# One list of pieces for a decoder layer's attention, with the work before and after it put between

## The reference, cut to what matters

```python
qkv = tgt @ qkv_w.T + qkv_b                      # tgt = layernorm(x), per entry 512 x 128
q, k, v = split(qkv, 3)
scores = (q k^T) * sqrt(128); all but the diagonal = -inf; attn = softmax(scores)
x1 = ln(tgt + (attn @ v) @ sa_out_w.T + sa_out_b) * ln1_g + ln1_b
# cross attention, 8 heads of 16, over 154 context rows per entry
ca = softmax(heads(x1 @ wq.T + bq) heads(mem @ wk.T + bk)^T / 4) heads(mem @ wv.T + bv)
x2 = ln(x1 + ca @ mha_out_w.T + mha_out_b) * ln2_g + ln2_b
x3 = ln(x2 + relu(x2 @ lin1_w.T + lin1_b) @ lin2_w.T + lin2_b) * ln3_g + ln3_b
x = x + tanh(g_xattn[3]) * x3
```

## Time and profile before

| what | value |
|---|---|
| median of 3 runs | 1736.38 us (1730.84 to 1736.41) |
| the profiled execution | 1737.62 us, its span 1735.8 us |
| PE busy over the span | 1430.0 us (82%) |
| DVE busy | 1154.2 us (66%) |
| GpSimd busy | 816.3 us (47%) |
| ACT busy | 767.0 us (44%) |
| granted PE clock, mean | 0.907 |

### The profile page before, as it was taken

One profiled execution on the slowest core, in us unless ns is written; L12 is line 12 of the kernel. 1 busy time (PEld: TensorE's weight loads), 2 busy tenths in 40 slices (PEclk: granted clock), 3 DMA queues, 4 the chain that ended last, 5 costly groups with the idle time before them and its releaser, 6 DMA issues.

```text
span 1735.8 us, 36462 instructions
## 1 busy us (share of the span) xinstructions
PE 1430.0 (82%) x13597; PEld 973.2 (56%) x13597; DVE 1154.2 (66%) x3020; ACT 767.0 (44%) x1520; POOL 816.3 (47%) x1236
## 2 busy tenths in 40 slices
PE   3999999999999986766798599869984885669997
PEld 2777777777777674644665255524443333425545
DVE  4888688877877764554856667554556565787754
ACT  3777677767766653411233355443212542201111
POOL 4789889978766872561336632000001301143330
PEclk9999999999999997965899899989986887879898
DMA  7332321211211202320000000000000000000000
GB/s 268 88 95 87 91 87 48 59 42 46 53 49 42 61 22 77 111 97 0 1 1 1 12 5 2 1 1 1 1 1 0 1 1 1 1 1 1 7 7 13
DMA packets 35477, 64.27 MB, mean 37 GB/s; under 512 B 7536, under 2 KB 25043, under 8 KB 34148
## 3 DMA queue, kind: packets, MB, share of 16 engines
q1 hardware_dynamic: 33831, 59.82, 11.6%
q0 software_dynamic: 1472, 2.12, 0.4%
HBM read 30.64 MB, written 12.66 MB: 25 GB/s over the span
## 4 chain that ended last, share of the span: by engine, by line
PE 62%; DVE 20%; ACT 6%; POOL 5%; issue 5%; DMA 2%; SPq 0%; ACTq 0%; DVEq 0%; POOLq 0%
PE banks L505 17%; PE banks L745 6%; PE banks L773 5%; PE banks L734 5%; PE banks L2145 4%; DVE xn L451 2%; PE banks L2131 2%; PE banks L480 2%; ACT work L932 2%; PE banks L2838 2%; PE banks L2098 1%; DVE norm_room L415 1%; PE banks L2781 1%; DMA work<-work 1%; POOL work L1040 1%
## 5 line engine op out<-in xcount | busy, mean ns | idle before, releaser
L1040 POOL TENSOR_TENSOR work<-work 128x512 bf16<-128x512 f32 (+1 forms) x512 | 359.6, 726 | 74.1 <-ACT work L932 73.3
L817 DVE TENSOR_REDUCE work<-banks 128x1 f32<-128x666 f32 x256 | 216.3, 845 | 67.6 <-PE banks L734 65.9
L445 POOL TENSOR_TENSOR norm_room<-norm_room,minus_half 128x4 f32<-128x4 f32 x48 | 50.2, 1046 | 408.3 <-DVE norm_room L420 392.9
L939 ACT ACTIVATE work<-banks,work 128x666 f32<-128x666 f32 x256 | 208.3, 814 | 36.5 <-DVE work L817 28.5
L932 ACT ACTIVATE work<-banks 128x512 f32<-128x512 f32 x256 | 152.9, 597 | 142.0 <-PE banks L745 141.7
L734 PE MATMUL banks<-work 128*128 128x512 bf16 (+1 forms) x1024 | 187.2, 305 | 6.8 <-DMA work<-work 6.4
L745 PE MATMUL banks<-const,work 128*128 128x128 f32 x1024 | 158.7, 278 | 14.7 <-ACT work L932 11.6
L505 PE MATMUL banks<-work,weights_b 128*128 128x512 bf16 (+1 forms) x840 | 159.6, 349 | 11.7 <-DVE work L2473 4.6
L734 PEld LDWEIGHTS banks<-work 128*128 128x128 bf16 x1024 | 95.6, 98 | 85.4 <-DMA work<-work 7.6
L773 PE MATMUL banks<-work 128*128 128x65 bf16 (+1 forms) x3840 | 136.5, 192 | 3.4 <-POOL work L1040 1.8
L480 PE MATMUL banks<-const,xn 128*128 128x128 f32 x176 | 39.4, 365 | 117.4 <-DVE xn L451 79.0
(11 more groups left out here) (441 smaller groups left out, 3231.7 us busy)
## 6 DMA issues: line engine op xcount, KB each, us to landing
work<-work SPq DMA_DIRECT2D x128, 166.5 KB, 2.9
sorted<-in_pads SPq DMA_DIRECT2D x10, 838.5 KB
weights_b<-in_weights SPq DMA_DIRECT2D x1, 4120.0 KB, 23.7
work<-scratch SPq DMA_DIRECT2D x64, 64.0 KB, 2.0
weights_b<-in_weights SPq DMA_DIRECT2D x1, 2824.0 KB, 9.4
weights_a<-in_weights SPq DMA_DIRECT2D x1, 2056.0 KB, 8.4
weights_a<-in_weights SPq DMA_DIRECT2D x1, 2050.0 KB, 10.1
work<-work SPq DMA_DIRECT2D x32, 64.0 KB, 1.9
```

Of the source, the lines that this page charges most:

```text
L817: ve.tensor_reduce(self.neg_max[i % 4], self.slot[i % 2][:, 0:KEYS0], AX_X, ALU.max, negate=True).then_inc(self.mark("max"))
L939: ac.activation(self.probs[i % 3], self.slot[i % 2][:, 0:KEYS0], ACT.Exp, bias=self.neg_max[i % 4]).then_inc(self.mark("exp"))
L1040: po.tensor_tensor(parts[:, :, :, 0], exact, parts[:, :, :, 1], ALU.subtract).then_inc(self.mark(event, i - 3))
```

## The change

Stage 6 becomes one list. `decoder_items` gives positions to all pieces of the layer: entry 0's first part at -4 to -2.9; for entries 1 to 3 the same pieces (`ahead`) from 2b - 2.0 on, 0.085 apart, so within the attention of the entry before; and for each unit, behind its output product at u + 2.56, the second norm, the feed-forward, the third norm and the sum into x (`measure2` to `close`), so within the attention of the next units. The router of entry 0 stands at 5.1 to 8.0. GpSimd walks the same list now.

In the pieces themselves: the bias of q and k comes into PSUM by a small bf16 matmul (`lead`, `in_bias6`) and ACT copies q and k out; the values are projected as columns, so that they need no transposes; the softmax's share goes into one scalar_tensor_tensor per tile with the residual; the gain and bias of the first two norms go into ACT's copy of the transposes (per-partition scale and shift), and for the rows themselves to GpSimd (`gain1`, `gain2`, `residual`, `x_base`), with the later biases added in the same pass; the third norm's gain, bias and gate are folded into two scalar_tensor_tensor per tile (`close`). All this works on halves of entries behind the attention. In stage 6 scores use two banks (0 and 1) in place of three; bank 2 serves the side work. `parts7` and its neighbours become one buffer per entry, of which stage 7 clears three on GpSimd at its start. In stage 4 the order of the pieces is what it was.

```diff
@@ context_memory
+        a.score_banks = 3 if heads == 16 else 2
@@ context_items
-        out, n = [], 2 * a.steps
+        out, n = [(-3.0, "key", 0, 0, 0), (-3.0, "key", 1, 0, 0), (-2.9, "query", 0, 0, 0), (-1.0, "out_bias", 7, 0, 0)], 2 * a.steps
+        for g in range(GROUPS):
+            out += [(-2.0 + 0.2 * g, "key_spread", g, 0, 0), (-1.9 + 0.2 * g, "rows", 0, g, 3 + g)]
+        if a.stage == 6:
+            out = self.decoder_items()
...
@@ context_pe, in the loop over the items (context_ac and context_ve likewise)
+            elif s == 6:
+                self.decoder_item_pe(pe, what, u, c)
...
@@ after context_ve
+    def key_bank(self, a, g, n):
+        return (2 * g + n + 5) % 8 if a.stage == 4 else 3 + (2 * g + n) % 4
@@ decoder
+    def decoder_items(self):
+        def ahead(b, at, step):
+            pieces = (("project", 0, 0), ("project", 1, 1), ("values6", 0, 2), ("dots", 0, 3), ("exp6", 0, 3.5), ("delta", 0, 4.5),
+                      ("attend", 0, 5), ("first", 0, 6), ("scale1", 0, 9), ("turn1", 0, 11))
+            return [(at + step * n, what, b, c, 0) for what, c, n in pieces]
+        out = [(-4.0, "start", 0, 0, 0)] + ahead(0, -4.0, 0.1)
+        out += [(-3.66, "key", 0, 0, 0), (-3.64, "key", 1, 0, 0), (-3.52, "out_bias", 6, 0, 0)]
+        out += [(-3.38 + 0.02 * g, "key_spread", g, 0, 0) for g in range(GROUPS)] + [(-3.3, "heads", 0, 0, 0)]
+        out += [(-2.8, "query", 0, 0, 0), (-1.0, "prepare", 0, 0, 0)] + [(-2.6 + 0.1 * g, "rows", 0, g, 3 + g) for g in range(GROUPS)]
+        for b in range(BATCH):
+            out += [(2 * b + 0.3 if b == 0 else 2 * b - 1.0, "gain1", b, 0, 0), (2 * b + 1.5, "x_base", b, 0, 0)]
+            if b:
+                out += [(2 * b - 2.1, "residual", b, 0, 0), (2 * b - 1.4, "heads", b, 0, 0)] + ahead(b, 2 * b - 2.0, 0.085)
+        for at, what in ((1.3, "measure"), (1.6, "scale"), (1.8, "turn")):
+            out.append((at, what, 5, BATCH - 1, 0))
+        for u in range(2 * BATCH):
+            for what, c, at in (("measure2", 0, 0.03), ("scale2", 0, 0.2), ("turn2", 0, 0.28), ("gain2", 0, 0.34), ("up", 0, 0.38), ("up", 1, 0.43),
+                                ("up", 2, 0.48), ("up", 3, 0.53), ("down", 0, 0.74), ("measure3", 0, 0.93), ("close", 0, 1.12)):
+                out.append((u + 2.56 + at, what, u, c, 0))
+            if u % 2 and u < 2 * BATCH - 1:
+                out += [(u + 2.56 + at, what, 6, u // 2, 0) for what, at in (("measure", 1.2), ("scale", 1.4), ("turn", 1.52))]
+        out += [(5.1, "squares", 0, 0, 0), (5.2, "logits", 0, 0, 0)] + [(5.4 + 0.2 * n, "router", 0, n, 0) for n in range(14)]
+        out += [(6.95, "router_exp", 0, 0, 0), (7.45, "router_turn", 0, 0, 0)]
+        return out
+    def half_room(self, u):
+        return self.room[:, 2 * BATCH + u // 2, ROOM * 2 * (u % 2):ROOM * 2 * (u % 2 + 1)]
+    def side6(self, b, c):
+        return c if b == 0 else (2, 7)[c]
 
@@ decoder_pe, decoder_item_pe (the loops removed stand in the kernel above)
...
+        self.context_pe(pe, self.decoder, lambda u: ("taken6", u))
+    def decoder_item_pe(self, pe, what, u, c):
+        w, y = self.w[6], self.xn
+        cols, tiles = slice(u * HALF, (u + 1) * HALF), y[:, 2 * u:2 * u + 2, :]
+        if what == "project":
+            bank = self.bank(pe, self.side6(u, c), "qkv_kept6", u, c)
+            self.columns(pe, 5, u)
+            for j in (0, 1):
+                t, out = QT * u + 2 * c + j, bank[:, j * 2 * P:(j + 1) * 2 * P]
+                pe.matmul(out, self.cb["lead"], self.in_bias6, start=True, stop=False)
+                m = pe.matmul(out, self.xt[:, t * P:(t + 1) * P], w["qkv"][:, 0:2 * P], start=False, stop=True)
+            m.then_inc(self.mark("projected6", u, c))
+        elif what == "values6":
+            bank = self.bank(pe, 2, "qkv_kept6", u, 2)
+            pe.matmul(bank, w["qkv"][:, 2 * P:3 * P], self.xt[:, self.cols_of(u)], start=True, stop=True).then_inc(self.mark("projected6", u, 2))
+        elif what == "attend":
+            bank = self.bank(pe, 2, "attended6", u)
+            pe.wait_ge(*self.at("qkv_kept6", u, 2))
             for j in range(QT):
+                m = pe.matmul(bank[:, j * P:(j + 1) * P], self.turned6[:, j * P:(j + 1) * P], w["sa_out"], start=True, stop=True)
+            m.then_inc(self.mark("brought6", u))
+        elif what == "turn1":
+            self.turn(pe, ("first", u), y[:, self.rows_of(u), :], 2, ("first", u))
+        elif what == "turn2":
+            self.turn(pe, ("second", u), tiles, 2, ("second", u))
+        elif what == "up":
+            bank = self.bank(pe, (2, 7)[c % 2], "relu6", u, c)
+            if c == 0:
+                pe.wait_ge(*self.at("columns", "second", u))
+            pe.matmul(bank[:, 0:HALF], w["lin1"][:, c * P:(c + 1) * P], self.xt[:, cols], start=True, stop=True).then_inc(self.mark("up6", u, c))
+        elif what == "down":
+            bank = self.bank(pe, 7, "fed6", u)
+            pe.wait_ge(*self.at("relu6", u, FT - 1))
+            for j in (0, 1):
                 for f in range(FT):
                     m = pe.matmul(bank[:, j * P:(j + 1) * P], self.hidden6[:, f, j * P:(j + 1) * P], w["lin2"][:, f * P:(f + 1) * P],
                                   start=f == 0, stop=f == FT - 1)
+            m.then_inc(self.mark("down6", u))
...
@@ decoder_item_ac (its relu and turns; the copies of the projection are alike)
+            ac.activation(self.qk6[c], self.bank_of(self.side6(u, c)), ACT.Copy).then_inc(self.mark("qkv_kept6", u, c))
...
+            self.turned(ac, ("first", u), self.xt[:, self.cols_of(u)], 2, SEQ, w["ln1_g"], w["ln1_b"])
...
+            ac.activation(self.hidden6[:, c, :], self.bank_of((2, 7)[c % 2], HALF), ACT.Relu, bias=w["lin1_b"][:, c:c + 1]).then_inc(self.mark("relu6", u, c))
@@ decoder_item_ve
+        if what == "dots":
+            for j in range(QT):
+                t, qk = QT * u + j, self.qk6[j // 2][:, j % 2 * 2 * P:(j % 2 + 1) * 2 * P]
+                ve.wait_ge(*self.at("qkv_kept6", u, j // 2))
+                i = ve.tensor_tensor_reduce(self.junk6[j], qk[:, 0:P], qk[:, P:2 * P], float(P) ** 0.5, 0.0, ALU.mult, ALU.add, score[:, t:t + 1])
+            i.then_inc(self.mark("dotted6", u))
+            ve.wait_ge(*self.at("dotted6", u))
+            ve.tensor_tensor(delta[:, own], score[:, own], score[:, own], ALU.subtract).then_inc(self.mark("delta6", u))
+        elif what == "delta":
+            ve.wait_ge(*self.at("exp6", u))
+            ve.wait_ge(*self.own("ve", ve.reciprocal(score[:, own], delta[:, own])))
+            ve.tensor_tensor(delta[:, own], delta[:, own], score[:, own], ALU.mult).then_inc(self.mark("shares6", u))
+        elif what == "first":
+            ve.wait_ge(*self.at("brought6", u))
+            ve.wait_ge(*self.at("x_based6", "residual", u))
+            ve.wait_ge(*self.at("shares6", u))
+            for j in range(QT):
+                t = QT * u + j
+                i = ve.scalar_tensor_tensor(y[:, t, :], self.bank_of(2)[:, j * P:(j + 1) * P], delta[:, t:t + 1], y[:, t, :], ALU.mult, ALU.add)
+            i.then_inc(self.mark("attended6", u))
+            ve.wait_ge(*self.at("attended6", u))
+            self.moments(ve, ("first", u), rows, room)
+        elif what == "scale1":
+            self.scale(ve, ("first", u), rows, rows, room)
+        elif what == "measure2":
             ve.wait_ge(*self.at("taken6", u))
+            self.moments(ve, ("second", u), rows, room, 2)
+        elif what == "scale2":
+            self.scale(ve, ("second", u), rows, rows, room, 2)
+        elif what == "measure3":
+            ve.wait_ge(*self.at("down6", u))
+            ve.wait_ge(*self.at("x_based6", "gain2", u))
+            ve.tensor_tensor(rows, self.bank_of(7, HALF).rearrange("p (t n) -> p t n", t=2), rows, ALU.add).then_inc(self.mark("fed6", u))
+            ve.wait_ge(*self.at("fed6", u))
+            self.moments(ve, ("close", 6, u), rows, room, 2)
+        elif what == "close":
+            _, mv, _, rstd = self.norm_room(room, 2)
+            ve.wait_ge(*self.at("x_based6", "x", u // 2))
+            for j in (0, 1):
+                i = ve.scalar_tensor_tensor(rows[:, j, :], rows[:, j, :], mv[:, j, 0:1], self.gain6, ALU.subtract, ALU.mult)
+            i.then_inc(self.mark("added6", u))
+            ve.wait_ge(*self.at("added6", u))
+            ve.wait_ge(*self.at("deviation", "close", 6, u))
+            for j in (0, 1):
+                x = self.x[:, 2 * u + j, :]
+                i = ve.scalar_tensor_tensor(x, rows[:, j, :], rstd[:, j:j + 1], x, ALU.mult, ALU.add)
+            if u % 2:
+                i.then_inc(self.mark("x6", u // 2))
+        elif what == "router":
+            if c == 0:
+                self.router_pieces = self.router_ve(ve, 0)
+            next(self.router_pieces, None)
@@ decoder_po
+    def decoder_rows_po(self, po, event, rows, gain, base):
+        wide = [P, rows.shape[1], P]
+        if gain is not None:
```

(44 more changed lines are left out.)

381 lines of the change are left out of this document (175 added, 206 removed).

## The result

The changed kernel takes 1752.55 us (median of 4 runs, 1750.01 to 1755.91), the kernel before beside it 1735.31 us (4 runs): ratio 1.009, 95% interval 1.0069 to 1.0111. It is 17 us slower; 1686 had been forecast, 50 faster. The profiled execution took 1755.91 us, its span is 1753.9.

A forecast was written before the change was run, and what follows sets the result against it. It took PE's queue to bound the attention, and step-by-step waits the stretches around it. Terms -36.2 (ahead), -69.2 (behind), +52.7 (middle), +2.6 (contention) gave -50.1, so 1686 us; own range 1674 to 1698, with rivals' near ends 1664 to 1708.

The forecast's parts named there:

- The sum of the parts moved: Within the attention: moved pieces add 52.7 us to PE, making 136.7, and bring DVE to 119.3.
- Tail: Behind the attention, last output product to stage 7's first product: 83.5 us becomes 14.3, so 69.2 less.
- 35 us of DVE passes: Whole stage 6: DVE loses 35 us of bias, gain and value passes, keeping its sum under PE's.
- The head: Ahead of the attention: only entry 0 remains, a 22.6 us chain to the first score, 36.2 us less.
- the 30 that it had named: Sign ahead of the attention: about 23 us from PE's first projection to first score, wrong if over 30.
- I take the holes as they are, 15.7 us: Within the attention: PE's idle time stays 15.7 us, half filled, as much added; middle 152.4 us.
- A middle over 170 us: Sign within the attention: 152 us expected to the last output product; over 170, the prediction is wrong as a whole.
- its rival with 0.99: Within the attention: holes fill and clock rises from 0.84 towards stage 4's 0.99; time 1676 or 1663, chance 0.23.
- Contention: Within the attention: GpSimd's bulk passes slow DVE's SBUF operations by 8 us, 2.6 of it on the path.
- Its sign for contention: Within the attention: DVE's 128x128 operations on `xn` at over 0.45 us each would speak for contention.
- Two banks: Stage 6 scores: two banks cost nothing if DVE is in time, at most 32 us; 3.5 taken.
- The rival "the engines take turns": Within the attention: each hop paid by both queues, middle 217.5 us, time 1749, slower; chance 0.03.

The follow-up runs named there:

- pieces_serial: Changed kernel with every entry's first part ahead of the attention, and all that follows output products, stage 7's layernorms and router behind it: 1736.36 us, ratio 0.9994.
- rows_off: Changed kernel with GpSimd's row passes cut to two columns of one tile, leaving their gains and biases out of the computation: 1755.7 us, ratio 1.011.
- spread: Changed kernel with other position numbers in `decoder_items` and nothing else, some handovers wider, others narrower: 1708.1 us, ratio 0.9815.

## Why the prediction was wrong

By its own steps:

- **The sum of the parts moved was right.** DVE's work in the middle: 119.3 forecast, 121.3 measured. Tail: 14.3 and 14.0. Three of its small sums are off by 0.1 to 0.2 (PE's parts per entry add to 5.5 and not 5.4, seven units to 29.4 and not 29.6, DVE's parts per entry to 5.6 and not 5.5), which changes nothing. Of the 35 us of DVE passes that the stage was to lose, 18.8 went by `pieces_serial`.
- **The head was 6.5 us short** (24.7 from the end of stage 5 to the first score; 31.2). From PE's first projection, at 1294.87, to the first score, at 1322.54, it is 27.7 for 22.6, so under the 30 that it had named. DVE and ACT ahead of the first score (time rows as above):

```profile
1291.01 2.90 DVE L455 TENSOR_SCALAR xn<-x,norm_room 128x128 f32<-128x128 f32 x4
...
1303.80 0.48 DVE L2222 TENSOR_TENSOR work<-work 128x308 bf16<-128x308 f32 x1 [1.85 <-ACT work L2189]
...
1307.25 2.14 DVE L2227 TENSOR_SCALAR work<-banks,const 128x308 bf16<-128x308 f32 x4
1309.31 2.44 DVE L455 TENSOR_SCALAR xn<-xn,norm_room 128x128 f32<-128x128 f32 x4
```

```profile
1301.45 1.28 ACT L2673 ACT_TABLE_LOAD   x1
```

  Four scalings took 2.90 and 2.44 us for 1.11 in the earlier trace rows. The first stands ahead of the projection, outside the chain; the second was in it at 1.1. The key adds (2.14) stand in DVE's queue ahead of the second, but GpSimd's power runs beside them until 1308.5, so that they cost 0.8. ACT's table load of 1.28 stands between the two key copies; the kernel before has one too, at 1300.10 us, in time in which ACT was idle. Neither was in the chain. `rows_off` shortens the head by 0.6 only: there the first takes 1.92 us and the second still 2.43.
- **The failed step: "I take the holes as they are, 15.7 us".** They were 58.2. It was reasoned from stage 4, which holds PE at 96% with the same list machinery. But what stands in that list beside the attention is less, and further apart: four layernorms have their transposes in the 123 us of the earlier trace rows, 0.22 to 0.6 positions behind their scaling, and PE waits for none of them there. Here the middle has 21 norms, and 14 sets of transposes 0.08 to 0.2 positions behind. The distances were held against each hop's own duration (3 us for 1.1), as if DVE began a piece at its position. The turn at 1418 us shows that it doesn't: from the end of an output product to the transposes that need it pass 9.0 us, of which 5.9 are other pieces ahead in DVE's queue, and PE's next items stand behind those transposes. `spread` shows that the places make the holes: the same pieces in other places, 24.9 us of holes less. A middle over 170 us was the prediction's own sign of being wrong as a whole.
- **The clock was left as it was.** The prediction knew that it could rise (its rival with 0.99) and didn't price that it falls. Of the middle's 55.8 us above 155.0, 39.9 are holes above 18.3 (15.7 and the 2.6 of contention), and 15.9 are PE's work, 152.6 for 136.7, at 0.77 instead of 0.84.
- **Contention: about right.** 8 us on DVE forecast, 6.4 and 6.3 measured by taking the row passes away. 2.6 on the path forecast; the holes fell by 3.7 and 2.4, but with the clock's part the time didn't fall. Its sign for contention (DVE's 128x128 operations on `xn` over 0.45 us) came, 481 ns for the scalings of `xn`; but these are still at 464 in `rows_off`, so not the row passes made them slow. Two banks: 3.5 allowed, nothing measured in the kernel before.
- **The rival "the engines take turns"** is what came: it had 217.5 for the middle and 1749 for the time; 210.8 and 1752.6 were measured. It got a chance of 0.03, because its threshold was put against hop lengths and not against DVE's queue. Its price had the right size by luck: it put all of DVE's new work, 65.1 us, in series with PE's 52.7, and no clock; measured are 42.5 us more of holes and 68.6 more of PE's work.
- **Stage 7** took 1.8 us more, near the 1.5 named for three clearings without cover; it was not tried apart.

What stays open: why the stages ahead of stage 6, with the same code, scatter by some 16 us between profiles, and how much of any ratio here is that. Which of the moves in `spread`, other than lin2's, take the holes away, and whether by distance or by what they no longer stand behind. And at which of the holes the clock falls: no run here tells single ones apart.

## What to carry to other kernels

Moving work into a stretch where the sum of every engine still fits is only half of an estimate; with queues in order, a piece also waits for what stands ahead of it in its engine's queue. A price for that would be the worst backlog of the engine that it goes to, left as distance before the next engine's piece that needs it; of such distances only lin2's was tried here by itself (0.6%). When an interleaved list gives nothing, change the distances before giving it up: here the same pieces went from 0.9% slower to 1.85% faster. And count PE's holes twice, once as they are and once in the clock of what stands between them.

## What was not expected of the hardware

- 946 matmul records of the same work took 152.6, 139.2 and 128.9 us at a granted clock of 0.77, 0.86 and 0.94. Idle products that filled some of the waits took 19 us off PE's other work (152.6 to 133.5).
- A kind of DVE operation with one SBUF input, the scaling of a 128x128 tile by two per-partition scalars, is slowed beside GpSimd's passes: four took 2.90 us, 1.92 with the row pass cut and other passes left, and 1.11 in the kernel before, with GpSimd idle. In the middle the 16 scalings of `x` take 539 ns each, and 341 in `rows_off`. The Trainium skill (GPSIMD Engine Reference, Specifications) counts instructions with two SBUF inputs or in a two-port mode; here the one-input scaling is hit as well, so by that page it would run in such a mode, which no run here shows.
- And still taking it away brought no time, neither in a kernel with 58 us of holes nor in one with 33: 3.7 and 2.4 us of holes went, and the granted clock fell from 0.77 to 0.74 and from 0.94 to 0.91. No run here says why.
